# A mixture-of-experts layer between two factored products: the values between the layers laid out token by token instead of 32 tokens innermost

## The reference

```python
def kmoe(x_flat, W_router, A, B, scale, bias, d_in1, d_in2, d_out1, d_out2, top_k):
    logits = x_flat @ W_router.T
    vals, idx = jax.lax.top_k(logits, top_k)
    probs = jax.nn.softmax(vals, axis=-1)
    xs = x_flat.reshape(-1, d_in1, d_in2)
    Y = jnp.einsum('nkoi,nij,nkpj->nkop', A[idx], xs, B[idx])
    out = jnp.einsum('nkop,nk->nop', Y, probs).reshape(-1, d_out1 * d_out2)
    return out * scale + bias
h = kmoe(x_flat, W_up, A_up, B_up, scale_up, bias_up, 32, 32, 64, 64, 2)
h = jax.nn.gelu(h, approximate=False)
y = kmoe(h, W_down, A_down, B_down, scale_down, bias_down, 64, 64, 32, 32, 2)
```

## Time and profile before

| | |
|---|---|
| median of three runs | 1257.72 us (1257.55 to 1258.91) |
| the profiled execution | 1257.94 us, its span 1255.9 us |
| PE busy | 1194.3 us, 95% of the span |
| PE weight loads | 797.9 us, 64% |
| DVE busy | 799.6 us, 64% |
| ACT busy | 435.9 us, 35% |
| POOL busy | 274.4 us, 22% |
| TensorE's granted clock, mean | 0.993 of full speed |
| stores of h and loads of h | 12 and 12 of 1024 KB, 4.4 and 5.1 us from issue to landing |

### The profile page before, as it was taken

One profiled execution on the slowest core, in us unless ns is written; L12 is line 12 of the kernel. 1 busy time (PEld: TensorE's weight loads), 2 busy tenths in 40 slices (PEclk: granted clock), 3 DMA queues, 4 the chain that ended last, 5 costly groups with the idle time before them and its releaser, 6 DMA issues.

```text
span 1255.9 us, 63911 instructions
## 1 busy us (share of the span) xinstructions
PE 1194.3 (95%) x28911; PEld 797.9 (64%) x28911; DVE 799.6 (64%) x1612; ACT 435.9 (35%) x894; POOL 274.4 (22%) x477
## 2 busy tenths in 40 slices
PE   9999999999999999999999999997898988899995
PEld 6865443444444334666676667766787877789995
DVE  5566787678767773355555555575848576467775
ACT  2322311131113212312221222235656556466664
POOL 1000000000000001112221222114443525245655
PEclk9999999999999999999999999999999999999998
DMA  7887999999999992510111011410413122143423
GB/s 286 277 273 229 313 321 308 303 305 329 301 322 299 321 334 94 120 68 0 67 67 67 7 59 50 126 41 14 166 60 134 67 95 106 38 132 113 122 58 77
DMA packets 64977, 203.09 MB, mean 162 GB/s; under 512 B 12112, under 2 KB 28496, under 8 KB 51440
## 3 DMA queue, kind: packets, MB, share of 16 engines
q1 hardware_dynamic: 64880, 201.77, 49.2%
HBM read 168.18 MB, written 33.55 MB: 161 GB/s over the span
## 4 chain that ended last, share of the span: by engine, by line
PE 84%; DVE 5%; issue 3%; SPq 2%; POOL 2%; DMA 2%; ACT 1%; POOLq 0%; DVEq 0%; ACTq 0%
PE ps L738 14%; PE ps L581 12%; PE ps L1111 9%; PE ps L2222 5%; PE ps L2305 5%; PE ps L2271 5%; PE ps L251 5%; PE ps L1225 4%; PE ps L1132 4%; PE ps L494 3%; PE ps L2200 2%; PE ps L2318 2%; PE ps L2257 2%; DVE arena L1956 2%; DVE arena L593 2%
## 5 line engine op out<-in xcount | busy, mean ns | idle before, releaser
L593 DVE STREAM_TRANSPOSE arena<-arena 128x448 f32<-128x448 f32 (+1 forms) x512 | 258.7, 574 | 54.9 <-DMA arena<-ctx 36.1
L581 PE MATMUL ps<-arena 32*64 32x400 f32 (+1 forms) x4096 | 188.7, 501 | 2.7 <-DVE arena L593 1.9
L738 PE MATMUL ps<-arena 128*64 128x512 f32 x832 | 189.1, 598 | 0.0
L581 PEld LDWEIGHTS ps<-arena 32*64 32x64 f32 x4096 | 81.8, 131 | 102.6 <-DVE arena L593 50.8
L616 ACT ACTIVATE arena<-ps,arena 128x384 f32<-128x384 f32 x64 | 36.3, 581 | 291.3 <-DVE arena L607 291.3
L738 PEld LDWEIGHTS ps<-arena 128*64 128x64 f32 x832 | 55.6, 136 | 121.3 <-issue 121.3
L1111 PE MATMUL ps<-arena 128*128 128x256 f32 x512 | 114.2, 381 | 0.8 <-ACT arena L1046 0.8
L1111 PEld LDWEIGHTS ps<-arena 128*128 128x128 f32 x512 | 96.4, 190 | 17.2 <-issue 3.3
L911 POOL TENSOR_TENSOR arena<-arena 128x1024 f32<-128x1024 f32 x8 | 18.9, 2367 | 390.5 <-PE ps L738 390.5
L2120 ACT COPY arena<-ps 128x512 f32<-128x512 f32 x128 | 75.0, 586 | 50.3 <-PE ps L2271 26.5
L1956 DVE SCALAR_TENSOR_TENSOR arena<-ps,arena 128x512 f32<-128x512 f32 x64 | 69.8, 1120 | 33.7 <-PE ps L2257 33.2
(11 more groups left out here) (161 smaller groups left out, 1882.6 us busy)
## 6 DMA issues: line engine op xcount, KB each, us to landing
arena<-ctx SPq DMA_DIRECT2D x64, 1024.0 KB
arena<-ctx SPq DMA_DIRECT2D x32, 768.0 KB
arena<-q_n SPq DMA_DIRECT2D x64, 256.0 KB, 11.3
h_n<-arena SPq DMA_DIRECT2D x12, 1024.0 KB, 4.4
arena<-h_n SPq DMA_DIRECT2D x12, 1024.0 KB, 5.1
arena<-x SPq DMA_DIRECT2D x16, 512.0 KB, 4.4
arena<-ctx SPq DMA_DIRECT2D x32, 256.0 KB
x_n<-arena SPq DMA_DIRECT2D x16, 512.0 KB, 3.5
```

The source lines that it names most:

```text
L581: last = pe.matmul(ps[b * SEQ:(b + 1) * SEQ, tb, 0:WIDTH[tb]], qs[p % 2][r, db, b * SEQ:(b + 1) * SEQ], z[PLACE[at]][r, b, 0:WIDTH[tb]], s ...
L593: vec.transpose(z[PLACE[at]][:, :, g * 224:g * 224 + nt * 32].rearrange("p b (j t) -> p b j t", t=32), slots[slot_of(k)][:, :, 0:nt, db * ...
L738: last = pe.matmul(ps[b * SEQ:(b + 1) * SEQ, OB, :], probt[:, j, b * SEQ:(b + 1) * SEQ], slot[:, b, jj, :], start=j == 0, stop=j == TILES - 1)
```

## The change

Inside a piece, h is laid out as `(n j)` instead of `(j n)`: the 64 columns of a token stand beside each other, and the next token follows. The views of h, and of the second buffer `hb` into which the pieces are loaded for the down half, are made so; every user follows. The writing of the bias, the Gelu and the read of `stage_h` now go over 8 (or 16) tokens of 64 words each, one run. The DMAs move the same bytes of a partition as one run. The moving operand of `logits_dn` becomes one word of each token, at a step of 64 words.

```diff
-    h = h_at.rearrange("p (q j n) -> p q j n", q=PIECE, j=F1)
-    hb = arena[:, hb_at:hb_at + 64 * P].rearrange("p (q j n) -> p q j n", q=PIECE, j=F1)
+    h = h_at.rearrange("p (q n j) -> p q n j", q=PIECE, j=F1)
+    hb = arena[:, hb_at:hb_at + 64 * P].rearrange("p (q n j) -> p q n j", q=PIECE, j=F1)
...
-            sp.dma_start(h_of[T][:, q].rearrange("p j n -> p (j n)"), a["h"][T, q, :, :]).then_inc(s_h[q], 16)
+            sp.dma_start(h_of[T][:, q].rearrange("p n j -> p (n j)"), a["h"][T, q, :, :]).then_inc(s_h[q], 16)
...
-                    sp.dma_start(a["h"][T, q, :, :], h[:, q].rearrange("p j n -> p (j n)")).then_inc(s_hd, 16)
+                    sp.dma_start(a["h"][T, q, :, :], h[:, q].rearrange("p n j -> p (n j)")).then_inc(s_hd, 16)
...
             vec.scalar_tensor_tensor(
-                h[:, q, :, at].rearrange("p j g -> p g j"),
+                h[:, q, at, :],
                 ps[:, b:b + 2, :].rearrange("p b (g x) -> p (b g) x", x=2 * F1)[:, :, 0:F1], scales[:, 0:1],
                 b_up.unsqueeze(1).to_broadcast([P, 8, F1]), ALU.mult, ALU.add).then_inc(s_bias, 1)
...
-            vec.tensor_copy(st_h[s % 2].rearrange("p (g j) -> p j g", g=8), h_of[T][:, q, :, at]).then_inc(s_sth, 1)
+            vec.tensor_copy(st_h[s % 2].rearrange("p (g j) -> p g j", g=8), h_of[T][:, q, at, :]).then_inc(s_sth, 1)
...
-            act.activation(h[:, q, :, at], h[:, q, :, at], ACT.Gelu).then_inc(s_gelu, 1)
+            act.activation(h[:, q, at, :], h[:, q, at, :], ACT.Gelu).then_inc(s_gelu, 1)
...
-            act.activation(h[:, q, :, two_at], h[:, q, :, two_at], ACT.Gelu).then_inc(s_gelu, 2)
+            act.activation(h[:, q, two_at, :], h[:, q, two_at, :], ACT.Gelu).then_inc(s_gelu, 2)
...
-                    last = pe.matmul(ps[half * E:(half + 1) * E, bank + t, 0:P], wr_dn[r, p, :], h[r, :, p, :],
+                    last = pe.matmul(ps[half * E:(half + 1) * E, bank + t, 0:P], wr_dn[r, p, :], h[r, :, :, p],
                                      start=p < 2, stop=p >= F1 - 2)
```

## The result

The changed kernel takes 1295.4 us as the median of four runs (1294.4 to 1296.1), against 1257.6 us in the four runs of the kernel before that stand beside it. The ratio is 1.0307, with a 95% interval of 1.0285 to 1.0329: 35.8 to 41.4 us more. Slower was forecast, by 26 us, so the direction is right and the size is not: the time lies above the forecast's own range of 1278 to 1290 us, and 0.6 us inside the margin to 1296 that was put on top of it.

What follows compares the result with a forecast made beforehand. PE was taken to bound the kernel, busy 95% of the span. 1255.9 - 2.3 (bias) + 28.4 (`logits_dn`) gave 1282.0 us of span, 1283.8 us measured time; own range 1278 to 1290, 8-in-10 range 1254 to 1296.

Steps and rivals of the forecast that it cites:

- What bounds the kernel: Whole kernel: PE busy 1194.3 of 1255.9 us sets the time, and nothing covers the 29.1 us of `logits_dn`.
- The DVE steps: Bias L1956 falls from 1120 to 686 ns, `stage_h` L1976 from 647 to 408, as words are written in runs.
- rival D: Bias L1956 does not get faster, its price being its repeated third operand; takes away the 2.3 us; chance 0.03.
- the forecast 686 from L979: Bias L1956 takes 686 ns, as does L979, the same operation and shape with a contiguous result.
- The 2.3 us on the path: Up half: the faster bias saves 0.3, 0.77, 0.77 and 0.45 us at the ends of the four turns.
- POOL's 3.2 us: Up half: PE's 3.2 us wait for POOL's L1853 stays, since POOL's own exponential stands ahead of it.
- `stage_h` and the Gelu at nothing: DVE's 15.3 us saved in `stage_h` and ACT's at most 1.1 us in the Gelu give nothing on the path.
- the allowance of 0.03 us for each Gelu: Gelu, 36 times on ACT: at most 0.03 us saved each, from L2125's 662 ns against the contiguous L1057's 631.
- the term for `logits_dn`: PE's moving operand in single words 64 apart costs 28.4 us more in four turns, between 24.2 and 32.6.
- Rival B: `logits_dn`: both column halves share one reader of a row, +94.4 us, 1349.8 us; chance 0.07 with everything over 1296.
- Rival A: `logits_dn`: PE reads single words at its pace, only the 2.3 us gain is left, 1255.4 us; chance 0.30.
- Rival C: `logits_dn`: a small PE price of 2 to 15 us, as if fetching ahead hid half, 1258 to 1270; chance 0.05.

Runs made afterwards that it cites:

- e2: The kernel before, with only `logits_dn` reading single words 64 apart (other values of h): 1300.3 us, ratio 1.0354 to the kernel before.
- e3: The kernel before, with only the bias rewritten to go over the 8 tokens innermost, layout and results kept: 1252.4 us, ratio 0.9972.
- e1: The changed kernel, with `logits_dn` reading four runs of 32 words again (other values of h): 1252.1 us against 1255.8 of the kernel before, ratio 0.9973.
- v5: The kernel before, with h laid out as 8 tokens, then 64 columns, then steps, every result kept: 1253.3 us against 1256.8, ratio 0.9970.
- e4: The kernel before, with only `stage_h` copying 512 words as one run (down half on another order of h): 1255.7 us, ratio 0.9995.
- v6: The changed kernel, with the two column halves reading columns 32 apart instead of neighbours: 1278.5 us, ratio 1.0167 to the kernel before.
- p2: The kernel before, `logits_dn` replaced by eight blocks using one, two or four array tiles: runs 7.1 to 1.8 us, single words 13.95 to about 4.4.
- p3: The kernel before, `logits_dn` replaced by ten single-word blocks, varying halves' distance and step: 4.32 us at 1 word apart, 3.49 to 3.52 from 4 on.
- p1: The kernel before, `logits_dn` replaced by ten blocks, each reading 128 words another way: runs 1.81 us a block, single words at step 64 4.58.

## Why the prediction was right and wrong

**What bounds the kernel** held. PE set the time, and `logits_dn` lay bare on its path: 45.3 us more there are 44.5 us more of kernel in e2.

**The DVE steps** held in kind. That the bias is slow because it writes words apart is shown by e3, which changes only the order of writing: 1120 to 746 ns. So rival D is out. 746 is 60 ns over the forecast 686 from L979; what these are is open. The 2.3 us on the path measured 3.4 us (1.6 to 5.0) in e1, 3.5 in e3 and 3.8 in v5. The second to fourth turns gave 1.0, 1.0 and 0.7 us, where 0.77, 0.77 and 0.45 were worked out, and the end of the first 0.46 (from L1522 to L2222, 2.91 us before and 2.45 after) for 0.3. All were a little small: the waits for DVE's later copies shrank as well. POOL's 3.2 us stayed, as said.

**`stage_h` and the Gelu at nothing**: right for both on the path (e4; v5 against e3). That L2131 would stay near 1112 ns was wrong, it took 1061; the allowance of 0.03 us for each Gelu came from L2125 alone.

**The step that failed** is the term for `logits_dn`: 28.4 us was taken, with bounds of 24.2 and 32.6 for the slow case, and it measured 45.3. It was right that PE's moving operand is slower in single words; the size was not right. The forecast took the middle of two prices carried over from DVE (its ratio of 1.83, and its 1.88 ns a word) and took the four streams as independent. The runs show 1.70 ns for a stream alone, 13.9 us a turn, and with the halves kept apart v6 has 14.2 us, 27.7 us more in four turns. So the price of a single word came out where the forecast put it. That is in part luck, since no run ties PE's price to DVE's.

What the sum lacked is the other 17.6 us, 4.4 a turn: a disturbance between the two column halves, which read the same partitions at a step of 64 and each time want two words of one 16-byte piece. Rival B came nearest to it, but its mechanism is refuted as it was put: a reader shared by the halves would slow them in p2's runs (3.5 us in two tiles, however they lie) and in p3 at 4 to 32 words apart (3.5 us), and neither is slow. Of its price 94.4 - 32.6 = 61.8 us were for the sharing; 17.6 were paid. It was given 0.07 and priced only in full, argued from DVE's two write streams, which are another engine's, and no small form of it went into the bounds of the forecast. A bound between the independent streams' 15.4 us a turn and the fully shared 30.9 would have held the 18.6.

**Rival A** is refuted by e1 and e2. Its best argument was L1225, whose words lie two apart. p1 agrees that two apart is nearly free (1.90 against 1.81 us), but four apart costs 3.65 us, so L1225 said nothing of larger steps. A stationary operand is free even at 64. **Rival C**'s price of 2 to 15 us did not come.

The rule of the Trainium skill, SBUF — State Buffer, in the section on the DMA port swizzle, two hits in a 16-byte line for full rate, holds for PE's moving operand: pairs 128 words apart run at nearly full pace in p1 (1.84 us a block against 1.81), single words from a step of 4 on do not (3.5 us and more).

**The sum of the changed kernel** from its parts: 45.3 from PE less 3.4 from DVE is 41.9 us, just above the measured 35.8 to 41.4. The long last turn's 2.7 us of issue time in the down loop would make it 39.2, inside. For v6 the same sum is 27.7 - 3.4 = 24.3 us, above its measured 18.3 to 23.6; less 2.4 us of issue time (0.8 for 3.2) it is 21.9, inside. That the 2.7 us are the long turn's doing rests on the issue rows of eight profiles, not on an experiment of their own, and why PE waits there stays open.

## What to carry to other kernels

Before turning a layout, list every reader and writer with the side that takes the step, and ask which of them is bare on the path: here four turns of PE paid for a saving that DVE had mostly hidden. In this kernel an operand could step at next to no cost where it moved on after pairs of words, and on two sides where single words were free too: DVE's read of PSUM and PE's stationary operand. Try first whether the order of one instruction's loops gives what the layout would be turned for, as it did in e3. When streams run beside each other, measure one alone, then two that share partitions, before multiplying.

## What the runs showed of the hardware that was not expected

- TensorE's moving operand of four-byte words takes 0.87 ns a word in runs, 0.9 in pairs or at a step of 2, and 1.70 alone at a step of 64; the last is 2.2 when the two column halves each time read two words of one 16-byte piece, and 1.7 again from 4 words apart on. At steps of 32, 48, 60, 62 and 63 neighbouring words cost 1.7 to 1.9.
- The stationary operand at a step of 64 words cost nothing: 1.84 us a block against 1.81, its weight load 131 ns as before.
- DVE's read of PSUM 128 words apart is free (746 ns in e3, as in the changed kernel). Its write to SBUF 32 words apart costs 374 ns for 512 words (1120 against 746).
- The Gelu of 1024 words got 51 ns faster in one run than in runs of 16: 1112 to 1061 ns.
